# Two groups' rows turned by 32x32 blocks on VectorE and transfers inside SBUF in place of TensorE transposes

## The reference

```python
q, k, v = x @ Wq, x @ Wk, x @ Wv
attn = softmax(einsum('btd,bTd->btT', q, k) * V ** -0.5)
attn_out = einsum('btT,bTd->btd', attn, v) @ Wp + bp
cms_out = gelu(attn_out @ cW1 + cb1) @ cW2 + cb2 + one_hot(target_codes)
modifier = gelu(concat([attn_out, cms_out]) @ mW1 + mb1) @ mW2 + mb2
x = clip(x + cms_out + modifier, 0, 1)
for layer in range(3):          # adapters, weights chosen by the sequence's role
    h = gelu(x @ W_down[role] + b_down[role])
    y = x + h @ W_up[role] + b_up[role]
    x = (y - mean(y)) * rsqrt(var(y) + 1e-5) * gamma[role] + beta[role]
```

## Time and profile before

| | before |
|---|---|
| median of three runs | 354.27 us |
| the profiled execution | 353.92 us |
| its span, first to last instruction | 352.1 us |
| TensorE busy | 340.7 us (97%) |
| VectorE busy | 203.2 us (58%) |
| ScalarE busy | 169.3 us (48%) |
| GpSimd busy | 61.2 us (17%) |
| granted TensorE clock | 1.00 |

### The profile page before, as it was taken

One profiled execution on the slowest core, in us unless ns is written; L12 is line 12 of the kernel. 1 busy time (PEld: TensorE's weight loads), 2 busy tenths in 40 slices (PEclk: granted clock), 3 DMA queues, 4 the chain that ended last, 5 costly groups with the idle time before them and its releaser, 6 DMA issues.

```text
span 352.1 us, 6686 instructions
## 1 busy us (share of the span) xinstructions
PE 340.7 (97%) x2259; PEld 283.5 (81%) x2259; DVE 203.2 (58%) x487; ACT 169.3 (48%) x337; POOL 61.2 (17%) x96
## 2 busy tenths in 40 slices
PE   6799999999999999999999999999999999999994
PEld 6686687788878888888877777877899999999962
DVE  6066367251353875466464665463689777454584
ACT  3465686464534544554254455353356454534421
POOL 2710140000040110001310110013221125100221
PEclk9999999999999999999999999999999999999999
DMA  6674799279110441200185997203867543298001
GB/s 215 187 237 149 183 124 145 26 165 164 32 60 0 118 120 31 96 30 15 54 279 154 264 290 238 61 32 99 207 151 207 146 128 84 70 290 329 20 0 45
DMA packets 32248, 46.14 MB, mean 131 GB/s; under 512 B 6396, under 2 KB 16950, under 8 KB 32214
## 3 DMA queue, kind: packets, MB, share of 16 engines
q1 hardware_dynamic: 30454, 41.72, 45.1%
q0 software_dynamic: 1392, 3.80, 3.7%
q10 hardware_dynamic: 368, 0.20, 0.2%
HBM read 43.60 MB, written 4.48 MB: 137 GB/s over the span
## 4 chain that ended last, share of the span: by engine, by line
PE 85%; DVE 5%; POOL 2%; ACT 2%; issue 2%; DMA 2%; SPq 0%; DVEq 0%; POOLq 0%
PE bank L331 12%; PE bank L333 12%; PE bank L332 12%; PE bank L1447 8%; PE bank L1452 8%; PE bank L1448 7%; PE bank L1491 4%; PE bank L1470 4%; PE bank L1351 2%; PE bank L1369 2%; PE bank L1309 2%; PE bank L1522 2%; DMA adapter_rows<-packed_rows 1%; PE bank L1570 1%; ACT h_full L811 1%
## 5 line engine op out<-in xcount | busy, mean ns | idle before, releaser
L811 ACT ACTIVATE h_full<-bank,bias 128x512 f32<-128x512 f32 (+1 forms) x80 | 48.2, 602 | 108.5 <-PE bank L333 103.0
L1043 DVE TENSOR_TENSOR h_lo<-h_full,h_hi 128x512 fp32r<-128x512 f32 (+1 forms) x80 | 46.7, 584 | 63.0 <-ACT h_hi L815 61.9
L731 POOL TENSOR_TENSOR rstd<-moments,minus_half 128x1 f32<-128x1 f32 x39 | 23.1, 591 | 169.6 <-DVE moments L1109 169.5
L815 ACT ACTIVATE h_hi<-h_full 128x512 fp32r<-128x512 f32 (+1 forms) x80 | 43.7, 546 | 2.5
L1101 DVE TENSOR_TENSOR window_y<-bank,window_x 128x256 f32<-128x256 f32 x39 | 16.5, 422 | 39.2 <-PE bank L1470 30.9
L1447 PE MATMUL bank<-h_hi,m_hi 128*128 128x512 f32 (+1 forms) x80 | 30.2, 387 | 0.2
L1447 PE MATMUL bank<-h_hi,c_hi 128*128 128x512 f32 (+1 forms) x80 | 30.2, 386 | 0.2
L331 PE MATMUL bank<-at_hi,c_hi 128*128 128x512 f32 (+1 forms) x80 | 29.3, 366 | 0.0
L331 PE MATMUL bank<-at_hi,m_hi 128*128 128x512 f32 (+1 forms) x80 | 29.1, 364 | 0.0
L333 PE MATMUL bank<-at_lo,c_hi 128*128 128x512 f32 (+1 forms) x80 | 27.8, 348 | 0.0
L333 PE MATMUL bank<-at_lo,m_hi 128*128 128x512 f32 (+1 forms) x80 | 27.8, 348 | 0.0
(11 more groups left out here) (237 smaller groups left out, 728.2 us busy)
## 6 DMA issues: line engine op xcount, KB each, us to landing
adapter_w<-packed_w SPq DMA_DIRECT2D x44, 256.5 KB, 3.5
adapter_rows<-packed_rows SPq DMA_DIRECT2D x36, 256.0 KB, 3.9
stage<-in_L_cond_mW SPq DMA_DIRECT2D x6, 512.0 KB, 4.5
mixed_w<-packed_w SPq DMA_DIRECT2D x8, 256.5 KB, 4.9
stage<-in_L_cond_cW SPq DMA_DIRECT2D x4, 512.0 KB, 5.8
last_w<-packed_w SPq DMA_DIRECT2D x2, 769.5 KB, 6.2
up_bias<-in_L_cond_b_up SPq DMA_DIRECT2D x12, 128.0 KB, 6.2
adapter_rows<-packed_rows SPq DMA_DIRECT2D x24, 64.0 KB, 2.2
```

The lines of the kernel that those rows point to most:

```text
L731: pool.tensor_tensor(slot.rstd[:, :], slot.moments[:, 1:2], minus_half[:, :], ALU.pow)\
L811: act.activation(h_full[:, n % 2, rows], bank[n % 2][:, rows], ACT.Gelu, bias=bias[:, b:b + 1])\
L815: act.activation(h_hi[:, n % 2, rows], h_full[:, n % 2, rows], ACT.Copy).then_inc(h_hi_ready, 1)
L1043: dve.tensor_tensor(h_lo[:, n % 2, rows], h_full[:, n % 2, rows], h_hi[:, n % 2, rows].bitcast(F32), ALU.subtract).then_inc(h_lo_ready, 1)
```

## The change

The transposes of groups 2 and 3 on TensorE and ScalarE's copies into xT are taken out. In their place stand, for each group, four new stages T0 to T3 on VectorE, one for each tile of 128 rows. T n turns the tile's 32x32 blocks with one `dve.transpose` of 128x256 into a buffer (`yz` for group 2, the windows' `y` tiles for group 3), reading features in steps of four. Four transfers on SyncE for each tile then put the blocks of each sequence into their place in xT, in pieces of 32 f32 values. Group 2's T0 to T3 stand at H4 to H7 of row group 0, group 3's at D10 to D13. VectorE's stages wait for the group's `x_in`, all four gathers. SyncE issues group 2's transfers ahead of `dbias`, and group 3's at the sixth item of its window loop. Group 3's rows are gathered twice: first, after `down_bias_done`, into the part of xT that will hold them turned, where T0 to T3 read them; later into `xr` as before, where Z reads them. ScalarE's X waits for all 16 transfers of the group (`x_spread`); VectorE waits for all 32 at H2 of row group 1, before the `y` tiles are used. The waits that X had on TensorE stand in Y.

```diff
+        def x_blocks(g, t):
+            return (attention(g).yz[:, :, :].rearrange("p k m -> p (k m)")[:, bass.ts(t, V)] if g == AHEAD
+                    else slots[t].y[:, :])
+
+        def x_raw(t):
+            return xT[:, t // 2, bass.ds((NG - 1) * GR + t % 2 * V, V)]
...
-        ATTENTION = {0: {("H", 10): ("X", 2), ("H", 12): ("Y", 2), ("H", 13): ("S", 2), ("H", 14): ("P", 2),
+        ATTENTION = {0: {("H", 4): ("T0", 2), ("H", 5): ("T1", 2), ("H", 6): ("T2", 2), ("H", 7): ("T3", 2),
+                         ("D", 10): ("T0", 3), ("D", 11): ("T1", 3), ("D", 12): ("T2", 3), ("D", 13): ("T3", 3),
+                         ("H", 10): ("X", 2), ("H", 12): ("Y", 2), ("H", 13): ("S", 2), ("H", 14): ("P", 2),
...
+            def spread_x(g):
+
+                for t in range(GT):
+                    sp.wait_ge(x_blocked, t + 1 if g == AHEAD else 2 * GT)
+                    for q in range(Q):
+                        sp.dma_start(xT[:, :, bass.ds(g * GR + t * P + q * T, T)],
+                                     x_blocks(g, t)[quarter(q), :].rearrange("p (f m) -> p f m", f=Q)).then_inc(x_spread, 16)
+
+            spread_x(AHEAD)
             sp.wait_ge(down_bias_ready, 1)
...
+                if n == len(WAVES[1]) + 1:
+                    spread_x(AHEAD + 1)
                 if 0 < n <= len(items) - len(ending):
                     window_rows(*items[n - 1][1:])
...
             gather(2)
+            pool.wait_ge(down_bias_done, 1)
+            for t in range(GT):
+                gather_rows(NG - 1, t, x_raw(t))
...
                 if stage_name == "X":
-                    act.wait_ge(xT_turned, g - AHEAD + 1)
+                    act.wait_ge(x_spread, 16 * Q * GT * (g - AHEAD + 1))
                     for vb in range(VB):
-                        act.activation(xT[:, vb, bass.ts(g, GR)], a.banks[vb][:, :], ACT.Copy).then_inc(xT_ready, 1)
-                    for vb in range(VB):
-                        act.wait_ge(xT_ready, 2 * VB * (g - AHEAD) + vb + 1)
                         act.activation(parts_hi[:, vb, :], xT[:, vb, bass.ts(g, GR)], ACT.Copy).then_inc(xT_ready, 1)
...
+                if stage_name[0] == "T":
+                    t = int(stage_name[1])
+                    rows = a.xr[:, t, :] if g == AHEAD else x_raw(t)
+                    dve.wait_ge(x_in[g], 16 * GT)
+                    if g == AHEAD:
+                        dve.wait_ge(at_done, VB)
+                    dve.transpose(x_blocks(g, t).rearrange("p (f k r) -> p k f r", f=Q, k=VB),
+                                  rows.rearrange("p (k i f) -> p k f i", k=VB, f=Q)).then_inc(x_blocked, 1)
...
+                if g == 1 and step == ("H", 2):
+                    dve.wait_ge(x_spread, 16 * Q * GT * (NG - AHEAD))
...
-                if stage_name == "X":
-                    pe.wait_ge(x_in[g], 16 * GT)
-                    if g > 1:
-                        pe.wait_ge(at_hi_ready, VB * (1 if g == 2 else 3))
-                        pe.wait_ge(at_lo_ready, VB * (1 if g == 2 else 3))
-                    for vb in range(VB):
-                        for i in range(GT):
-                            ins = pe.transpose(a.banks[vb][:, i * P:(i + 1) * P], a.xr[:, i, vb * P:(vb + 1) * P],
-                                               ident[:, :])
-                    ins.then_inc(xT_turned, 1)
                 if stage_name == "Y":
-                    pe.wait_ge(xT_ready, 2 * VB * (g - AHEAD + 1))
+                    pe.wait_ge(at_hi_ready, VB * (1 if g == AHEAD else g))
+                    pe.wait_ge(at_lo_ready, VB * (1 if g == AHEAD else g))
+                    pe.wait_ge(xT_ready, VB * (g - AHEAD + 1))
...
                     pe.wait_ge(pd_ready, g + 1)
+                    if g == NG - 1:
+                        pe.wait_ge(x_in[g], 16 * GT * 2)
```

More of the change, by code:

```diff
@@ L290, in build @@
         half_y_ready = sem("half_y_ready")
-        xT_turned = sem("xT_turned")
+        x_blocked = sem("x_blocked")
+        x_spread = sem("x_spread")
         xT_ready = sem("xT_ready")
@@ L699, in _, with gather_rows @@
             pool.wait_ge(rows_known, 1)
+            def gather_rows(g, t, o):
+                pool.indirect_dma_start(out=o, out_offset=None, in_=x_rows,
+                                        in_offset=bass.IndirectOffsetOnAxis(ap=row_idx[:, g * GT + t:g * GT + t + 1], axis=0))\
+                    .then_inc(x_in[g] if g >= AHEAD else half_in[2 * g + t // (GT // 2)], 16)
             def gather(g):
                 for t in range(GT):
[L703 to L706, removed]
+                    gather_rows(g, t, attention(g).xr[:, t, :])
             def store(x_tile, w, counter):
@@ L1004, in attention_part @@
                     for vb in range(VB):
-                        dve.wait_ge(xT_ready, 2 * VB * (g - AHEAD) + VB + vb + 1)
+                        dve.wait_ge(xT_ready, VB * (g - AHEAD) + vb + 1)
                         dve.tensor_tensor(parts_lo[:, vb, :], xT[:, vb, bass.ts(g, GR)], parts_hi[:, vb, :].bitcast(F32),
                                           ALU.subtract).then_inc(xT_lo_ready, 1)
+                if stage_name[0] == "T":
[6 more added lines that the diff above has]
+                                  rows.rearrange("p (k i f) -> p k f i", k=VB, f=Q)).then_inc(x_blocked, 1)
                 if stage_name == "Z" and g >= AHEAD:
```

## The result

The changed kernel takes 365.45 us (median of six runs, 363.27 to 367.12) against 354.31 for the kernel before: ratio 1.0306, 95% interval 1.0285 to 1.0326. The profiled execution took 365.61 us with a span of 363.8. The prediction was 365.2 with a range of 361 to 369.

A forecast was written before the change was run, and what follows sets the result against it. TensorE, busy 340.7 of 352.1 us, was taken as the bound. From 353.92, less 1.67 for the transposes, plus 10.9 of stop and 2.0 of pace loss, came 365.15, so 365.2 us, range 361 to 369.

The forecast's parts named there:

- The moved wait: VectorE at T0 of group 2 waits for all four gathers, landing 63.3; TensorE stops at 53.59 for 10.9 us.
- the bounds 61.1 and 64.55: Group 2's landing in the new kernel: 61.1 as the third gather, 64.55 as the fourth before; 63.3 taken.
- The pace after the stop: TensorE behind the stop runs at half pace until the clock is back: 2.0 us lost, 0 if it doesn't fall.
- Rival 1: TensorE's stop comes but its clock stays up: 363.2 us; chance 0.15.
- The upper end of the forecast, 367.5: Forecast case, stop with pace loss, put at 362.3 to 367.5 us; chance 0.63.
- The gain: 16 transposes removed from TensorE, eight at 69.31 and eight at 120.42: 1.67 us; ScalarE's copies worth nothing by themselves.
- The transposes on VectorE: Eight added 128x256 transposes on VectorE, 0.44 us taken for each, bounds 0.30 and 0.85.
- The transfers: 32 added transfers inside SBUF, 16 a group: about 10 us a group, at most 21; covered at 10.
- 5.3 for 16: Issuing one group's 16 transfers on SyncE: about 0.33 us each, 5.3 us in all.
- Rival 3: Stop plus slow 128-byte pieces; ScalarE at X or VectorE at H2 of group 1 late 1 to 5: 366 to 370; chance 0.12.
- After the stop: T3 ends 7.6 us after T0; cms could start at landing + 9.2 by TensorE, + 7.6 by VectorE: nothing more lost.
- Rival 2: Group 2's rows are there in time, landing up to 52.4, no stop: 352.3 us; chance 0.08.

The follow-up runs named there:

- experiment 5: Changed kernel plus 44 extra identity multiplications on TensorE ahead of its wait for h_lo of H5: 362.28 us, ratio 1.0234 to the kernel before.
- experiment 4: Changed kernel with gathers left in place, group 2's T0 to T3 together behind H9 and X at H11: 360.14 us, ratio 1.0157.
- experiment 2: Group 2's gathers issued earlier, once Z of group 1 is done: changed kernel 352.13 us (0.9952), kernel before with the same move 353.79 (0.9999).
- Experiment 3: Changed kernel with group 2 turned on TensorE as before, only group 3's part in: 353.35 us against 354.38, ratio 0.9974.
- experiment 1: Group 2's gathers issued as soon as Z of group 0 is done: changed kernel 358.57 us (1.0102), kernel before with the same move 359.56 (1.0141).

## Why the prediction was right, point by point
**The moved wait.** Right in its place and in its chain: T0 behind chunk 6, released by DMA, then h_lo of H5, then TensorE at the second half of D5. The stop was put at 10.9 us and measured at 10.79. Two small errors cancel in it. T0 began at 63.94, which less the 0.82 us of that execution's late start is 63.1 in place of 63.3; and from there to TensorE's matmul it took 1.26 us (65.20 - 63.94) in place of 1.15. The fourth gather, issued at 48.76, landed after

```profile
DMA to landing us min/median/max: 15.2/15.2/15.2
```

where the earlier trace rows has 16.6, so it was 1.4 us quicker (14.9 in the trace of experiment 5, which has the same order of transfers). The prediction had put in 1.25 for the dbias transfers that no longer lie beside it; that these are the cause was argued and not tried. That the choice between the bounds 61.1 and 64.55 came out this close is in part luck.

**The pace after the stop.** 2.0 in the sum, 2.03 in the trace, 1.91 by experiment 5. Rival 1 falls: the clock does fall. The way from the kernel's first rows to this number was thin: the earlier trace rows has the double spacing, but the same trace gives 1.00 as the granted clock from 4.86 to 7.60, so that those rows were at half clock isn't shown. The 2.0 was a choice between 0 and 2.9, and it came out well in part by luck. The Trainium skill's rule ("TensorE: Matmul & The Clock Gate", HAM oscillation), by which a burst of matmuls behind a wait for DMA starts at the lower clock, is borne out by the trace: clock 0.50 from 65 to 69 after the stop of 10.8 us. It was low after the wait of 4.76 us in experiment 4 as well. (The upper end of the forecast, 367.5, is 0.25 more than its terms add up to.)

**The gain.** 1.67 us put on the 16 transposes; the shifts in the trace fell by 0.93 and 0.91, in all 1.84, and experiment 2 measured 1.66. That two copies on ScalarE for each group went as well added nothing, as TensorE didn't wait for them in the trace of before; no run takes them out alone.

**The transposes on VectorE.** Put at 0.44 us; the view of their line shows 0.63, with starts 0.56 apart before the next instruction. This term was too low by 0.12 to 0.19, inside the bounds 0.30 to 0.85. It cost nothing where it is covered.

```profile
L1037 DVE STREAM_TRANSPOSE yz<-xr x4: 628/632/634, 63.9 to 72.8; 128x256 f32<-128x256 f32 x4
L1037 DVE STREAM_TRANSPOSE window_y<-xT x4: 620/626/650, 91.0 to 107.5; 128x256 f32<-128x256 f32 x4
```

**The transfers.** The size was wrong, and no harm came of it in the changed kernel. An issue of such a transfer takes SyncE 0.61 us and more, not 0.33:

```profile
L581 SPq DMA_DIRECT2D xT<-yz x16: 610/614/745, 64.6 to 75.5; - x16
L581 SPq DMA_DIRECT2D xT<-window_y x16: 612/614/727, 108.1 to 118.1; - x16
```

Sixteen take 10.6 us, so the issuing and not the moving sets the end. The step that failed is "5.3 for 16", taken from the shortest issues of the window loads (0.33 in the trace of before), though the earlier trace rows has 0.75 and 1.0 us for an issue too. The moving is far cheaper than its bound. From 108 to 121 us that queue has

```profile
q1 hardware_dynamic: 4352, 0.53, 26.8%
```

that is 13 us x 16 x 0.268 / 4352 = 13 ns of an engine for a packet, against the 83 ns of the average one in the earlier trace rows. By the byte these pieces are still the slower ones: 128 bytes in 13 ns are about 10 bytes a nanosecond of an engine, where the average packet of the earlier trace rows has about 17. This agrees in direction with the 512-byte mark of the Trainium skill ("DMA: Bandwidth & Descriptors", Specifications), but the issuing, not this rate, set the time. Rival 3 didn't come about: neither X on ScalarE nor H2 of group 1 on VectorE was late for these transfers in the changed kernel. Group 3's last issue ends at 118.7 and VectorE's wait for it stands at 120.2, so the cover was 1.5 us less what a landing takes, where 2 to 3 had been thought; experiment 4 shows what issuing them costs where nothing covers it (11.1 us there). Experiment 3 shows no cost for group 3, within its interval.

**After the stop.** That the steps behind it cost nothing more was right, the margin wasn't. The prediction had T3 end 7.6 us after T0 began and TensorE 1.6 us later. T3 ended 9.5 us after it, and VectorE went straight on to cms, without idle time:

```profile
72.82 0.63 DVE L1037 STREAM_TRANSPOSE yz<-xr 128x256 f32<-128x256 f32 x1
73.38 1.24 DVE L1082 TENSOR_TENSOR cms<-bank,cms_bias 128x512 f32<-128x512 f32 x2
```

So VectorE, and not TensorE, was the later one at step C, by about 0.1 us: cms is 13.75 after its old place, where D6 was 13.64 late. VectorE had lost its lead to the slow clock and the longer transposes: it waited 1.31 us for ScalarE at the h_lo of H7 (70.40), and ScalarE had waited for TensorE. The 0.1 was covered, as the first matmul that reads cms_hi came at 75.72, 13.64 after its old place.

**Rival 2** (the rows are there in time, 352.3 us) didn't come about, but its price was right: experiment 2 made its condition true and gave 352.13, beside 353.80 for the kernel before.

## What to carry to other kernels
When a reader of gathered or loaded data is moved forward, look up when the data lands and not when it is issued, and take the last of all transfers that its semaphore counts; the time of landing is invisible in the old kernel as long as the old reader comes later. On an in-order engine the price is not the moved instruction's but that of everything behind it, and a stop of TensorE cost its length plus about 2 to 2.6 us of low clock behind it in these runs. Transfers also cost the engine that issues them: 16 took 10.6 us of SyncE, and that needs cover as well. Before giving up such a move, look for a quieter place for the transfer: here one of 10 us earlier turned a loss of 3% into a gain of 0.5%.

## What the runs showed of the hardware
- A wait of 4.76 us of TensorE (experiment 4) was enough for the granted clock to fall from 2.4 to 1.2 GHz; after 10.8 us it fell too, and in both it was low for some 4 to 6 us of work behind the wait. A wait of 2.1 us in experiment 1 had the clock fall in one trace (2.10 us, then 0.50 until about 40) and not in the other (2.06 us, then 1.00). A wait of 0.52 us behind 88 small matmuls left it at 1.0 (experiment 5).
- Four indirect gathers issued beside a dense run of 128x32 matmuls and a softmax on VectorE cost 5.2 us, though no semaphore links them; issued 5.5 us later they cost nothing (353.79 against 353.80). The cause stays open.
- A transfer inside SBUF with 128-byte pieces costs the issuing engine 0.61 us and more, nearly twice the 0.33 us of an issue of a window's rows, and the DMA engines 13 ns a packet, about 10 bytes a nanosecond of one engine.
